# Down projection of a fused layer: high and low products summed in one PSUM bank

## The reference, cut to what matters

```
x = x + chunked_linear_attention(layernorm(x))      # "attn_a", 4 heads, chunks of 128
x = x + ffn(layernorm(x))                           # first feed-forward
x = x + softmax_attention(layernorm(x))             # "attn_b", one head of 512
x = x + ffn(layernorm(x))                           # second feed-forward, same weights

def ffn(x):      # HID = 1408, DIM = 512
    W(wq, s) = (wq - 128) * s[:, None]              # integer codes 0..63, one scale per row
    gate = silu(x @ W(wq_gate, s_gate).T)
    up   = x @ W(wq_up, s_up).T
    return (gate * up) @ W(wq_down, s_down).T       # the down stage; s_down is one scale per output
```

## Time and profile before

| | us |
|---|---|
| median of 3 runs | 952.7 (952.39 to 952.9) |
| the profiled execution | 952.1 |
| its span in the trace | 950.4 |

### The profile page before, as it was taken

One profiled execution on the slowest core, in us unless ns is written; L12 is line 12 of the kernel. 1 busy time (PEld: TensorE's weight loads), 2 busy tenths in 40 slices (PEclk: granted clock), 3 DMA queues, 4 the chain that ended last, 5 costly groups with the idle time before them and its releaser, 6 DMA issues.

```text
span 950.4 us, 13242 instructions
## 1 busy us (share of the span) xinstructions
PE 935.8 (98%) x4691; PEld 529.5 (56%) x4707; DVE 617.3 (65%) x1138; ACT 457.1 (48%) x912; POOL 476.7 (50%) x487
## 2 busy tenths in 40 slices
PE   7999999999999999999999999999999999999998
PEld 4888988888744444444444455445455444444444
DVE  7555647859777668776855466445476777676644
ACT  4443334356577535664433354323455665356631
POOL 5433424477266676666840043304333466665574
PEclk9999999999999999999999999999999999999999
DMA  9401300024200220014000000000000002410001
GB/s 318 179 5 34 133 23 23 2 89 142 92 34 1 45 45 1 1 23 67 1 0 1 1 1 1 0 1 1 1 1 1 1 1 37 97 45 1 1 22 67
DMA packets 64801, 36.59 MB, mean 38 GB/s; under 512 B 52000, under 2 KB 52320, under 8 KB 64736
## 3 DMA queue, kind: packets, MB, share of 16 engines
q1 hardware_dynamic: 64736, 35.74, 12.9%
HBM read 28.36 MB, written 7.37 MB: 38 GB/s over the span
## 4 chain that ended last, share of the span: by engine, by line
PE 93%; DVE 2%; ACT 2%; POOL 1%; DMA 1%; SPq 1%; issue 1%; DVEq 0%; POOLq 0%
PE psum L2216 54%; PE psum L2463 14%; PE psum L2465 13%; PE psum L2603 7%; PE psum L2265 1%; PE psum L2614 1%; DMA bq_col<-bq 1%; PE psum L2350 1%; PE psum L2254 1%; ACT probs L1417 0%; DVE xb_lo L2121 0%; ACT xb_hi L1423 0%; DVE ln_bn L1532 0%; SPq L681 0%; POOL wvT_lo L1001 0%
## 5 line engine op out<-in xcount | busy, mean ns | idle before, releaser
L943 POOL TENSOR_TENSOR hid<-hid,hid_hi 128x512 f32<-128x512 f32 x88 | 102.6, 1166 | 102.8 <-DVE hid_hi L1883 102.8
L2463 PE MATMUL psum<-xf,w_gu 128*128 128x512 f16 x352 | 133.8, 380 | 0.0
L2463 PE MATMUL psum<-xf,w_s 128*128 128x512 f16 x264 | 100.0, 379 | 1.5 <-DVE up L1856 1.3
L2465 PE MATMUL psum<-xf,w_gu 128*128 128x512 f16 x264 | 100.1, 379 | 0.0
L1278 ACT ACTIVATE hid_lo<-hid 128x512 f16<-128x512 f32 x88 | 55.0, 625 | 33.0 <-POOL hid L943 33.0
L939 POOL TENSOR_TENSOR hid<-up,gate 128x512 f32<-128x512 f32 x44 | 56.0, 1272 | 22.9 <-ACT gate L1273 22.9
L2465 PE MATMUL psum<-xq,w_s 128*128 128x512 f16 x176 | 66.7, 379 | 0.0
L2463 PEld LDWEIGHTS psum<-xf,w_gu 128*128 128x128 f16 x352 | 34.3, 98 | 53.9 <-ACT acc L1263 15.5
L1273 ACT ACTIVATE gate<-gate,sg_xs 128x512 f32<-128x512 f32 x44 | 31.7, 721 | 63.3 <-DVE gate L1866 63.3
L805 POOL TENSOR_TENSOR xrstd<-xvar,minus_half 128x1 f32<-128x1 f32 x48 | 25.5, 550 | 59.2 <-DVE xvar L1536 59.2
L1883 DVE TENSOR_SCALAR hid_hi<-hid 128x512 f16<-128x512 f32 x88 | 39.1, 444 | 16.0 <-POOL hid L939 14.5
(11 more groups left out here) (330 smaller groups left out, 2548.1 us busy)
## 6 DMA issues: line engine op xcount, KB each, us to landing
cla_wide<-cla_dram SPq DMA_DIRECT2D x16, 256.0 KB, 3.3
out<-xres SPq DMA_DIRECT2D x15, 256.0 KB, 2.0
xres<-x SPq DMA_DIRECT2D x3, 1024.0 KB, 12.8
turned<-blocks SPq DMA_DIRECT2D x24, 128.0 KB, 3.1
codes_gu<-gateT SPq DMA_DIRECT2D x1, 2816.0 KB, 11.7
codes_gu<-upT SPq DMA_DIRECT2D x1, 2816.0 KB, 11.1
codes_da<-downT SPq DMA_DIRECT2D x1, 1536.0 KB, 7.0
blocks<-xn SPq DMA_DIRECT2D x12, 128.0 KB, 2.6
```

Source lines behind the costliest of these rows:

```text
L943: nc.gpsimd.tensor_tensor(hid[:, :], hid[:, :], hid_part(hid_hi, j, half), ALU.subtract).then_inc(rest_done, 1)
L2463: nc.tensor.matmul(bank(use[0]), w, x_operand(piece, k, False), start=start and k == 0, stop=False, skip_group_check=not start)
L2465: last = nc.tensor.matmul(bank(use[0]), w, x_operand(piece, k, True), start=False, stop=k == 1, skip_group_check=not start)
```

## The change

All products of one tile now go to one bank. The low products use a second copy of the down weights, scaled by 2^-11, so that they can be added to the high products where they stand.

```diff
-    def down_hi(t):
-        return (5, t // 2) if t % 2 == 0 else (7, t // 2)
-    def down_lo(t):
-        return (6, t // 2) if t % 2 == 0 else (2, JT + t // 2)
+    def down_use(t):
+        return ((5, t // 4), (7, t // 4), (6, t // 4), (2, JT + t // 4))[t % 4]
+    def w_down_low(j):
+        return cols(wd_low, j) if j < JT - 1 else wd_low_last[:, :]
```

```diff
+LOW_TILES = {0: {8: ((0, 2),), 9: ((2, 4),), 10: ((4, 5), (5, 6)), 11: ((6, 8), (8, 10))},
+             2: {3: ((0, 2),), 4: ((2, 4),), 5: ((4, 5), (5, 6)), 6: ((6, 8),), 7: ((8, 10),)}}
+LOW_STEPS = tuple(sum(len(v) for v in LOW_TILES[blk].values()) for blk in (0, 2))
...
+                def low_weights(first, end):
+                    w = wd_a[:, first * D:end * D] if first < 5 else wd_b[:, (first - 5) * D:(end - 5) * D]
+                    nc.scalar.activation(wd_low[:, first * D:end * D], w, ACT.Copy,
+                                         scale=1.0 / LO).then_inc(wd_low_done, 1)
...
+                    for first, end in LOW_TILES.get(blk, {}).get(j, ()):
+                        if (blk, first) == (0, 0):
+                            act.wait_ge(wvo_out, 16)
+                        if blk == 0 and first == 0:
+                            act.wait_ge(wd_ready_pool, 5)
+                        low_weights(first, end)
```

TensorE waits for all six writes of the block's copy (`wd_low_done`) before the first low product, and does high before low:

```diff
+                        if low and t == 0 and j == 0:
+                            pe.wait_ge(wd_low_done, LOW_STEPS[0] + LOW_STEPS[1] * (blk // 2))
+                        if low and t == 0 and j == JT - 1:
+                            pe.wait_ge(wd_low_last_done, blk + 1)
...
-                down(0, down_lo(0), hid_lo, most)
+                down(0, False, most)
                 part(4, j, alpha(j, 3), False)
                 part(3, j, delta(j, 1), False)
-                down(0, down_hi(0), hid_hi, most)
-                down(1, down_lo(1), hid_lo, most)
-                down(1, down_hi(1), hid_hi, most)
+                down(0, True, most)
+                down(1, False, most)
+                down(1, True, most)
```

```diff
+            def weights_out():
+                for v_use in V_USE:
+                    Use(sp, "mid", 0).read_out(v_use)
+                sp.wait_ge(mid_hi_done, 2 * KT)
+                sp.dma_start(wvo_dram, wvo[:, :]).then_inc(wvo_out, 16)
+            def weights_back():
+                Use(sp, "F1", 1).full(down_use(LAST))
+                sp.dma_start(wvo[:, :], wvo_dram).then_inc(wvo_in, 16)
```

The outputs are read from PSUM by VectorE alone, which multiplies by `sd_rows` and adds to the residual. ScalarE's copies to `y_low` and all of GpSimd's work on outputs are gone, in all four blocks:

```diff
-                    nc.scalar.activation(y_low[t % 2][:, :], bank(down_lo(t)[0]), ACT.Copy,
-                                         scale=1.0 / LO).then_inc(drained[down_lo(t)[0]], 1)
-                    nc.gpsimd.tensor_tensor(cols(yt, t % 2), cols(yt, t % 2), sd_rows[:, :],
-                                            ALU.mult).then_inc(y_scaled, 1)
-                    nc.vector.tensor_tensor(cols(yt, t % 2), bank(down_hi(t)[0]), y_low[t % 2][:, :],
-                                            ALU.add).then_inc(drained[down_hi(t)[0]], 1)
+                    nc.vector.tensor_tensor(cols(yt, t % 2), bank(down_use(t)[0]), sd_rows[:, :],
+                                            ALU.mult).then_inc(drained[down_use(t)[0]], 1)
```

More of the change, by code:

```diff
@@ L238, in hybrid_layer_kernel @@
     xn_pair = [xn, yt]
-    y_low = [at("y_low0", Z + 102400, D), at("y_low1", Z + 69632, D)]
+    wd_low = at("wd_low", Z + 94208, (JT - 1) * D, BF16)
+    wd_low_last = at("wd_low_last", Z + 69632, D, BF16)
     qk_hi = at("qk_hi", R1, 2 * KT * D, F32R)
@@ L252, in hybrid_layer_kernel @@
     g_lo = at("g_lo", Z + 90112, KT * D, F16)
-    wvo_hi = at("wvo_hi", Z + 94208, KT * D, F16)
-    wvo_lo = at("wvo_lo", Z + 98304, KT * D, F16)
+    wvo = at("wvo", Z + 94208, 2 * KT * D, F16)
+    wvo_hi, wvo_lo = wvo[:, 0:KT * D], wvo[:, KT * D:2 * KT * D]
     mid_sq = at("mid_sq", Z + 102400, D)
@@ L787, in _ @@
                 blocks_to_turned(q, 0, 1)
+                if q == B0:
+                    weights_back()
             store(0, *range(BT))
@@ L1307, in ffn @@
                             x_copy(NEXT_SET[blk], i)
[L1308 to L1315, removed]
+                        x_highs(NEXT_SET[blk], i)
+                        x_34_high(NEXT_SET[blk], i)
             um = Use(act, "mid", 0)
@@ L1907, in ffn @@
                     if b == 1 and j == 0:
-                        x_34_low(BLOCK_SET[blk], 3)
                         add_y(blk - 1, BT - 1)
@@ L1920, in ffn @@
                         high(hid1, hid1_hi_done, j - 1, 0)
+                    if j == JT:
+                        nc.vector.tensor_scalar(wd_low_last[:, :], w_down(JT - 1), 1.0 / LO, None,
+                                                ALU.mult).then_inc(wd_low_last_done, 1)
                     extra(j)
@@ L1947, in last_rows @@
                         dve.wait_ge(last_hi, i + 1)
[L1948 to L1952 removed]
+                        nc.vector.tensor_tensor(xs[:, c], xs[:, c], cols(yt, LAST % 2)[:, c],
                                                 ALU.add).then_inc(x_updated, 1)
@@ L2467, in part, with down_product, down @@
                     last.then_inc(filled[use[0]], 1)
-                def down(t, use, hid, js):
+                def down_product(t, c, use, low, j, start, stop):
+                    o = j * BTOK + t * P
+                    hid, w = (hid_lo, w_down_low(j)) if low else (hid_hi, w_down(j))
+                    return mm(bank(use[0])[:, c], hid[:, o:o + P], w[:, c], start, stop)
+                def down(t, low, js, end=False):
+                    use = down_use(t)
                     for j in js:
-                        if j == 0:
+                        if j == 0 and not low:
@@ L2472, in down @@
                             u.free(use)
-                        pe.wait_ge((hid1_lo_done, hid2_lo_done)[t // 4], JT * blk + j + 1)
-                        o = j * BTOK + t * P
-                        last = mm(bank(use[0]), hid[:, o:o + P], w_down(j), j == 0, j == JT - 1)
-                    if js[-1] == JT - 1:
+                        if low:
+                            pe.wait_ge((hid1_lo_done, hid2_lo_done)[t // 4], JT * blk + j + 1)
+                        else:
+                            pe.wait_ge((hid1_hi_done, hid2_hi_done)[t // 4], JT * blk + j + 1)
@@ L2477, in down @@
+                        if low and t == 0 and j == 0:
+                            pe.wait_ge(wd_low_done, LOW_STEPS[0] + LOW_STEPS[1] * (blk // 2))
+                        if low and t == 0 and j == JT - 1:
+                            pe.wait_ge(wd_low_last_done, blk + 1)
+                        last = down_product(t, slice(0, D), use, low, j, j == 0 and not low, end and j == js[-1])
+                    if end:
                         last.then_inc(filled[use[0]], 1)
                 def last_halves():
-                    u.free(LAST_HI[0])
@@ L2481, in last_halves @@
-                    u.free(LAST_HI[1])
-                    for c, use in zip(HALVES, LAST_HI):
-                        for j in range(JT):
-                            o = j * BTOK + LAST * P
-                            last = mm(bank(use[0])[:, c], hid_hi[:, o:o + P], w_down(j)[:, c], j == 0, j == JT - 1)
+                    u.free(LAST_USES[0])
+                    u.free(LAST_USES[1])
+                    for c, use in zip(HALVES, LAST_USES):
+                        for low in (False, True):
+                            for j in range(JT):
+                                last = down_product(LAST, c, use, low, j, not low and j == 0, low and j == JT - 1)
```

106 lines of the change are left out of this document (30 added, 76 removed).

## The result

The changed kernel takes 956.06 us (median of 6 runs, 955.5 to 956.78) against 952.6 (6 runs beside it, 952.39 to 952.96): ratio 1.0037, 95% interval 1.0026 to 1.0048. It is 3.5 us slower, 2.5 to 4.6 by the interval. The profiled execution took 955.9 us with a span of 954.1, 3.7 more than before's 950.4.

The account below looks back on a forecast made before the run. TensorE, busy 98% of the span, bounds the kernel. Terms +3.1 - 0.85 - 0.3 + 0.2 + 0.0 = +2.1 gave 954.2 on the profiled execution, 954.8 us on the median; range 953.4 to 957.2.

Parts of the forecast that it names:

- the rival with the lower clock: Behind block 0's gap, matmuls begin at the lower clock level, costing 1.4 us more: 956.2 us in all; chance 13%.
- The wait in block 0, +3.1: TensorE's first low product waits 3.1 us for ScalarE's last two wd_low pieces behind low(hid2, 9); bounds 2.3 and 4.0.
- Short pieces: Rival: ScalarE's big pieces in block 0 cost nearer 0.63 us, so the wait is 2.3 us, total 954.0; chance 10%.
- the wait isn't there: Rival: block 0's last two pieces run in ScalarE's 2.73 us idle time, so TensorE doesn't wait: 951.8 us; chance 7%.
- The tail, -0.85: Kernel's end: without low steps, VectorE reads the last product about 0.04 us behind TensorE, gaining 0.85 us.
- `part(6)` waits for GpSimd, -0.3: At two block borders, part(6) no longer waits for GpSimd's last low part of pair 3: gain 0.3 us.
- `part(2)` waits for bank 2, +0.2: At two block borders, the next block's part(2) waits for VectorE to read tile 7 from bank 2: loss 0.2 us.
- Pair 3 late, bounds 0 to 3.3, taken as 0: Pairs after tiles 4 and 5 cost nothing; rival: 0.5 us in each of three blocks, 956.3 us, chance 12%.
- ScalarE's copies, cost to TensorE taken as nothing: Readout: ScalarE's 32 copies leave; TensorE did not wait for them, so nothing is gained except at three places.
- The other pieces: Earlier wd_low pieces in blocks 0 and 2 fit ScalarE's idle time ahead of silu2: zero cost.
- both DMAs: Sending wvo out and back for stage B, 5.4 us each, has about 5 us of cover: zero cost.
- the last tile's halves: In the last tile, 22 products of 256 columns take 2.42 us against 2.38 for 11 of 512: no change.

Follow-up runs that it names:

- The first experiment: Changed kernel with the last two pieces of block 0's scaled weight copy moved ahead of low(hid2, 9) on ScalarE: 951.18 us, ratio 0.9985 to before.
- the fourth: Kernel before plus two unused 1024-column ScalarE copies behind low(hid2, 9) in block 0 and TensorE's wait for them: 957.0 us, ratio 1.0041.
- filled gap: Changed kernel with 15 spare 512-column matmuls ahead of block 0's first low product, so TensorE works during the wait: 953.98 us, ratio 1.0018 to before.
- shorter gap: Changed kernel with only one of the two late copy pieces moved ahead of low(hid2, 9), the other left behind it: 954.16 us, ratio 1.0018 to before.
- the fifth: The first experiment's kernel with banks 2 and 6 exchanged, so tile 7 stands in bank 6: 950.88 us, ratio 0.9981 to before.
- sixth: The fifth's kernel with X_AFTER = (1, 3, 5, 6) as in the kernel before, the last two pairs one tile later: 950.44 us, ratio 0.9978 to before.
- The last experiment: Kernel before with tile 0's last low product moved ahead of tile 1's high products: 951.64 us, ratio 0.9994.

## Why the prediction was right and where it was not

The forecast was 954.8 us with a range of 953.4 to 957.2; the result is 956.06. The direction and the main mechanism, the wait, were right. But the time lies next to 956.2, which was the rival with the lower clock, at a chance of 13%, and the trace says that this rival held: its sign, the granted clock behind the gap, came out against the forecast. By its steps:

- **The wait in block 0, +3.1:** right. 3.26 us by the starts, 3.10 as the list has it. The piece, bounded by 0.63 and 1.50 and taken at 1.03, took (1.99 + 0.10) / 2 = 1.04 us. *Short pieces* and *the wait isn't there* fall. The Trainium skill, "ScalarE: Activation LUTs", What ACT_TABLE_LOAD costs, gives 186 ns + 0.833 ns per column, an estimate of 1.04 us: the trace agrees, for bfloat16 input too. The first experiment shows that the wait's removal removes the loss, the fourth that the wait alone makes it.
- **The clock, 13% at +1.4:** this is the step that failed, and it cost most. The rival was true: 1.53 us behind the gap, shown from three sides (filled gap: nothing; shorter gap: 1.59; wait alone: 1.57). My argument against it was that the earlier trace rows show the engine's first work, not a pause in full work. That distinguished two cases without a row that showed them to differ. The Trainium skill, "TensorE: Matmul & The Clock Gate", Why this matters for your kernels, warned of idle gaps between bursts; the trace agrees with it for 3.10 us, and traces here show the fall behind shorter pauses than the page warns of (2.15, 2.01 and 1.86 us, last section). The figure read from the start-up rows (1.4) was good to 0.2 us.
- **The tail, -0.85:** right. From the end of the last matmul to the start of VectorE's last reading of its bank it is 947.36 - 946.47 = 0.89 us before and 951.12 - 951.08 = 0.04 after: -0.85.
- **`part(6)` waits for GpSimd, -0.3:** the step is a plain one in the changed kernel (370.84 to 371.06), at both borders, but the mechanism was wrong, and the number is luck. `part(6)` waits for two engines. In before GpSimd ended at 365.91, and ScalarE's `first_sum(0)`, which frees the bank, at 365.36 + 0.58 = 365.94:

```profile
365.36 0.58 ACT L1251 ACTIVATE acc<-psum 128x512 f32<-128x512 f32 x1
```

  TensorE started at 366.09, 0.15 behind ScalarE, as it did by 0.14 in the fifth and sixth kernels, where GpSimd was done 5.4 and 1.7 us before the start. So it was ScalarE that ended this wait. In the changed kernel the step is plain because TensorE has already lost the time at `part(2)`, four matmuls earlier.
- **`part(2)` waits for bank 2, +0.2:** right, and a little small: the step is 0.38 (369.81 to 370.19), 0.16 too long, at both borders 0.33. The two terms are one delay in two places: from the first matmul of the block to the first of `part(6)` it is 1.90 us in both kernels (366.09 - 364.19 and 371.06 - 369.16). The border gained nothing and lost nothing; with another bank for tile 7 it is 1.80 (366.19 - 364.39).
- **Pair 3 late, bounds 0 to 3.3, taken as 0:** between. One of three blocks shows it, and not in every execution. In the changed kernel, TensorE and VectorE at pair 3 of block 1:

```profile
466.27 1.35 PE L2240 MATMUL psum<-ident,xn 128*128 128x128 f32 x8
467.68 1.03 PE L2191 MATMUL psum<-wd_a,hid_hi 128*128 128x512 bf16 x4
...
465.47 1.45 DVE L1534 TENSOR_SCALAR xn<-xres,xmv,xrstd 128x512 f32<-128x512 f32 x2
```

  1.41 us from the first turn to the next product's record, less 0.22 for the one record missing of five, less the 0.88 without a wait: 0.3 late. In the first and third experiments, which have the same order there, the same distance is 1.09 less 0.22, so nothing is late, and in the fifth it is late again. The rival's 1.5 us did not come.
- **ScalarE's copies, cost to TensorE taken as nothing:** wrong, and not named. "TensorE did not wait for them" overlooked bank 6: 0.21 us in each block, 0.8 in all. I had looked for idle time of TensorE, where a step that is 0.2 us too long does not show, since a matmul lasts 0.38 and the next one is due after 0.216. The last experiment shows the wait itself, since its step is gone in all four blocks; what the total gains by it stayed within the noise.
- **The other pieces, both DMAs, the last tile's halves, at nothing:** right. There is one wait on `wd_low` in the list, none on the values weights, and stage B differs by 0.04. `wvo` came back in 4.7 us behind its issue at 477.15, and the queries ran until 487.32.

The sum as measured on the spans: wait +3.26, clock +1.53, borders 0, pair 3 +0.3, tail -0.85, bank 6 -0.84, start-up +0.36: +3.76 against 954.1 - 950.4 = 3.7. The items below 0.4 are close to what one trace can tell.

Three errors thus lie in a forecast that was 1.3 us low: the clock (+1.5) and pair 3 (+0.3) left out on one side, bank 6 (-0.8) on the other. That they partly cancel is luck.

## What to carry to other kernels

Where a change makes a saturated TensorE wait for some microseconds in the middle, add what the matmuls behind the gap lose by the lower clock to the wait itself; a wait of 3.3 us cost 4.8, and pauses of about 2 us lost the same 1.6 behind them where the clock fell. Before a large buffer's last pieces are put at the end of another engine's list, look for idle time of that engine a few instructions earlier: moving two copies ahead of one turned 0.4% slower into 0.15% faster. Look for waits on a pipelined engine in the distance of starts, not in idle time alone. And where a wait vanishes, measure from a fixed point ahead of it to one behind it: here one step became plain because another, four matmuls earlier, had become longer.

## What the hardware showed that I had not expected

- Pauses of TensorE much shorter than 3 us dropped its clock in some executions. In the traces here the granted clock fell to the lower level behind idle times of 3.15, 3.10, 2.15, 2.01 and 1.86 us, with 1.5 to 1.6 us lost behind each, and did not fall behind 1.60 (pairs later), 1.34 (changed kernel) and 1.29 us (before). At 2.15 us about half of the executions show a mean clock that speaks for a fall. The length of the pause alone may not decide; no run here varies it finely. Before, early in the kernel:

```profile
18.45 0.50 PE L2216 MATMUL psum<-wv_hi,xt_hi 128*128 128x512 f32 x1 [1.29 <-ACT ab_row L1137]
...
19.25 0.39 PE L2216 MATMUL psum<-wv_hi,xt_hi 128*128 128x512 f32 x1
```

- The start-up differs between executions by more than the effects studied here, and the two traces with a late start show the same fall of the clock. The same place in the first experiment, whose block 0 began 3.0 us later, and its stretch of 2 us behind the pause (granted clock 0.58):

```profile
19.86 0.50 PE L2194 MATMUL psum<-wv_hi,xt_hi 128*128 128x512 f32 x1 [2.01 <-ACT ab_row L1134]
...
20.92 0.63 PE L2194 MATMUL psum<-wv_hi,xt_hi 128*128 128x512 f32 x1
...
24.40 0.42 PE L2293 MATMUL psum<-ident,ab_row 16*128 16x16 f32 x4
```

```profile
20.00:22.00 2.00, 2.00 (x6) 1.57 (x7) 2.00 (x3) 0.38 (x2) 0.44 (x1) 0.58 1.05 389
```

  The pause ended 1.41 us later than before (19.86 against 18.45): TensorE waits there for `ab_row`, and ScalarE's operation that makes it waits for the DMA of `bq`. From there to the transposes of `ab_row` it takes 24.40 - 19.86 = 4.54 us at the lower clock, where before takes 21.39 - 18.45 = 2.94: 1.60 more. Together that is the 3.0 us. The last experiment's trace shows the same: a pause of 1.86 us ending at 19.04, then the lower clock, and block 0 2.2 us late. Of the 56 executions of the kernel before beside the experiments, the three with a mean clock under 0.999 took 954.53 to 954.92 us, where the medians are 952.39 and 952.52; but two others are as slow (954.47 and 954.72) at 1.000 and 0.999, so other causes remain. It is why the table above is cut by blocks, and why medians, not one span, carry the ratios.
